# Linear attention on TensorE: from two streams to four, with head features, scores and state product in other pieces

## The chip, the cores and the metric

The kernel runs on one core of a Trainium2 chip. The metric is the time on the device in microseconds (us); lower is better. Everything is float32.

## What is computed

The program is a two-layer network over x of 8 batches, 1024 tokens and 128 features. The first layer (a recurrent mixer and a mixture of experts) and the gather of weight tiles that closes the second layer are the same before and after. The change is in the attention of the second layer, which runs three times over (L=3), causally over 1024 tokens, with 16 heads of 8 features, and then a feed-forward part of width 512:

```python
h = _layernorm(x, axis=-1) * (1 + ca) + sa
# favor(x, omega), 8 features out of 8 for each head
xs = x * dh ** (-0.25)
u = jnp.einsum('bshd,dm->bshm', xs, omega)
h = 0.5 * jnp.sum(xs * xs, axis=-1, keepdims=True)
return jnp.concatenate([jnp.exp(u - h), jnp.exp(-u - h)], axis=-1) * m ** (-0.5)
# one layer
q = (out @ Wq[l] + bq[l]).reshape(B, S, N_HEAD, dh)   # k, v likewise
Qf = favor(q, omega[l])
Kf = favor(k, omega[l])
a = causal_linear_attention(Qf, Kf, v).reshape(B, S, D)
a = a @ Wo[l] + bo[l]
h = layer_norm(out + a, ln1_g[l], ln1_b[l])
y = jax.nn.relu(h @ W1[l] + bf1[l]) @ W2[l] + bf2[l]
out = layer_norm(h + y, ln2_g[l], ln2_b[l])
```

## The kernel before

The attention works in 48 jobs. A job is one layer for 512 tokens (half a batch, four blocks of 128). Its running sum over tokens (`carry`) goes on to the other half of the batch, and its output to the next layer. Two streams s=0 and s=1 hold the buffers of two jobs (`at_xn0`, `at_xn1`, ...), and jobs of the two streams take turns. Every engine runs a hand-written sequence, `slot(a, f, then)`, once for each pair of jobs: job a does its first half (projections, features, sums, scores, weighting), the job before it, f, its second half (output projection, first layer norm, feed-forward, second layer norm), and `then` is the job that comes next. Engines meet by semaphores (`wait_ge`, `then_inc`); PSUM has eight banks of 128x512, four for each stream.

In one job, with the names of the buffers:

- TensorE turns the input (`transposed_input`, L1840, `at_xn`); ScalarE copies it out as `at_xT` (L1679). The first matmul of the slot, keys, is L1928; values L1929. Each is one matmul of 128x128 by 512 columns, which the profile shows as two records (x2).
- Head features: `omega` is folded into Wk and Wq once at the start (`feature_weights`, `at_wu`), so that u is one full matmul from `at_xT` (L1934, L1937 or L1938 for the queries' side) and minus the half square another with the constant `half` on `at_sqk` or `at_sqq`. With two matmuls for each of keys and queries these are four of 512 columns. ScalarE takes the exponential; queries come in four masked copies (L1669, `at_qa`), keys as `at_kb` by four products with masks on VectorE (L1543).
- `sums` (L1847): products of keys by token with values in tiles of 32x32. VectorE picks the blocks of a head out of them (L1553, state terms) and runs the prefix sum over the blocks (L1559).
- `scores` (L1859) come in two halves with half of `feed_forward_out` (L1890) after each; `causal` (L1565) masks each on VectorE. `carried` (L1868), the state product, is queries times state in two tiles of 64x64 on the diagonal, and `weighed` (L1875) scores times values, each half after its `causal`. VectorE divides (L1519) and turns the result.
- `output_weights` (L1882), sum and first layer norm (L346, L349, L368), feed-forward in four matmuls (L1965) and out in sixteen (L1890), second sum (L1576) and layer norm, whose output is the input of the job of the next layer, two slots later. Of layer 0 the input is the modulated layer norm of x instead; all of its steps were on VectorE.

After the last job, VectorE prepares the gather stage (`tiles_ahead`: L1460, L1442) in slot 48 and GpSimd writes the last rows (L1763 to L1769); tile rows are then loaded, normalised (L1637) and multiplied.

## Time and profile before

| | |
|---|---|
| median of 3 runs | 1801.85 us (1801.15 to 1805.26) |
| span of the profiled execution | 1828.0 us, granted TensorE clock 0.916 in the mean |
| TensorE matmul busy | 1571.7 us (86% of the span) |
| VectorE busy | 1443.5 us (79%) |
| ScalarE busy | 935.3 us (51%) |
| GpSimd busy | 698.6 us (38%) |

The runs are timed without the profiler; the profiled execution's own time is its span, 1828.0 us, 1.5% over the median. The attention's jobs lie from 520 us to about 1740 us of it. Busy is time in which at least one instruction runs; the rest is waiting or issue.

### The profile page before, as it was taken

How to read it: one execution, taken by the hardware profiler on the slowest of the kernel's cores; microseconds unless marked ns; L12 is line 12 of the kernel's file. 1: busy time of each engine (PE TensorE's matmuls, PEld its weight loads, DVE VectorE, ACT ScalarE, POOL GpSimd, SP SyncE). 2: the span in 40 equal slices, each digit the busy share in tenths (PEclk: the TensorE clock that was granted, in tenths of full speed). 3: DMA queues.
4: the chain of work that ended last, by engine and by line, in shares of the span. 5: the costliest groups of instructions: out<-in, count | busy, mean ns of one | idle time of the engine just before them, and what ended most of it. 6: DMA issues, size and time to landing. Idle time of an engine off the chain costs nothing.

```text
span 1828.0 us, 65037 instructions
## 1 busy us (share of the span) xinstructions
PE 1571.7 (86%) x27934; PEld 1150.5 (63%) x27934; DVE 1443.5 (79%) x3906; ACT 935.3 (51%) x1958; POOL 698.6 (38%) x620
## 2 busy tenths in 40 slices
PE   6777365399969999999999999999999999999853
PEld 4344254399946677776667777666677667777542
DVE  4998566766658888888888888888888988888864
ACT  4887476366524444445544444554444544444373
POOL 0777636345513234215224323423321522431354
PEclk9888655599969999999999999999999999999876
DMA  9730012333200000000000000100000000000437
GB/s 264 145 100 1 21 50 90 97 102 101 83 13 14 3 9 9 15 3 14 15 3 13 16 3 8 20 3 9 9 15 3 14 15 3 11 6 3 109 102 233
DMA packets 88606, 79.69 MB, mean 44 GB/s; under 512 B 22416, under 2 KB 77040, under 8 KB 88064
## 3 DMA queue, kind: packets, MB, share of 16 engines
q1 hardware_dynamic: 70736, 46.17, 9.6%
q0 software_dynamic: 10848, 25.70, 4.9%
q8 instruction: 221, 3.62, 0.9%
q10 hardware_dynamic: 6736, 3.66, 0.7%
q14 instruction: 65, 0.53, 0.1%
HBM read 46.74 MB, written 34.01 MB: 44 GB/s over the span
## 4 chain that ended last, share of the span: by engine, by line
PE 50%; DVE 13%; ACT 4%; issue 2%; DMA 1%; DVEq 1%; POOL 0%; another core or an unknown queue 0%; POOLq 0%; ACTq 0%
PE psum L1965 8%; PE psum L1890 8%; PE psum L1859 4%; PE psum L1868 4%; PE psum L1928 2%; PE psum L1934 2%; PE psum L1882 2%; PE psum L1936 2%; PE psum L1875 2%; PE psum L1937 2%; PE psum L1938 2%; PE psum L1948 2%; PE psum L1847 2%; DVE at_kb L1543 2%; PE psum L1929 2%
## 5 line engine op out<-in xcount | busy, mean ns | idle before, releaser
L1890 PE MATMUL psum<-attn_w,at_qa 128*128 128x128 f32 x1536 | 197.6, 282 | 0.0
L1752 POOL TENSOR_TENSOR at_xres<-at_xn,attn_rows 128x512 f32<-128x512 f32 x32 | 40.9, 1277 | 394.2 <-DVE at_xn L368 394.2
L1965 PE MATMUL psum<-at_vT,attn_w 128*128 128x512 f32 x384 | 180.6, 614 | 6.8 <-ACT at_vT L1697 5.8
L1890 PEld LDWEIGHTS psum<-attn_w,at_qa 128*128 128x128 f32 x1536 | 179.6, 192 | 6.1 <-issue 0.7
L1543 DVE TENSOR_SCALAR at_kb<-at_kf,const 128x512 f32<-128x512 f32 x192 | 178.4, 989 | 0.0
L1757 POOL TENSOR_TENSOR at_xn<-at_sqk,attn_rows 128x512 f32<-128x512 f32 x48 | 63.6, 1326 | 202.8 <-DVE at_sqk L368 202.8
L1549 DVE STREAM_TRANSPOSE at_vb<-at_vT 32x512 uint32<-32x512 uint32 x192 | 134.7, 701 | 1.9
L1669 ACT ACTIVATE at_qa<-at_qf,const 128x512 f32<-128x512 f32 x192 | 127.6, 714 | 1.6
L1713 ACT ACTIVATE at_qa<-psum,attn_bf 128x512 f32<-128x512 f32 x192 | 122.1, 678 | 10.6 <-PE psum L1965 5.4
L1565 DVE TENSOR_TENSOR at_weights<-psum,const 128x1024 f32<-128x1024 f32 x96 | 115.6, 1204 | 11.3 <-PE psum L1859 11.3
L361 ACT ACTIVATE at_rstd<-at_mv,const 128x4 f32<-128x4 f32 x96 | 28.1, 292 | 184.3 <-DVE at_mv L349 184.2
L1965 PEld LDWEIGHTS psum<-at_vT,attn_w 128*128 128x128 f32 x384 | 70.0, 192 | 82.2 <-issue 71.8
L1859 PE MATMUL psum<-at_qa,at_kb 64*64 64x64 f32 x6144 | 113.5, 224 | 9.5 <-issue 5.4
L1859 PEld LDWEIGHTS psum<-at_qa,at_kb 64*64 64x64 f32 x6144 | 100.5, 137 | 21.0 <-issue 9.9
L1868 PE MATMUL psum<-at_state,at_qa 64*64 64x36 f32 x3072 | 111.1, 242 | 0.0
L1868 PEld LDWEIGHTS psum<-at_state,at_qa 64*64 64x64 f32 x3072 | 106.3, 143 | 0.0
L1058 POOL DMA_INDIRECT token_y<-ex_y,ex_place x71 | 70.1, 988 | 85.3 <-DVE ex_y L1018 79.0
L1763 POOL TENSOR_TENSOR at_qf<-at_qf,ga_rows 128x512 f32<-128x512 f32 x16 | 20.3, 1271 | 207.8 <-DVE at_qf L368 207.8
L1847 PEld LDWEIGHTS psum<-at_v,at_kt 32*32 32x32 f32 x6144 | 62.1, 103 | 50.9 <-issue 49.4
L1049 POOL DMA_INDIRECT sorted_x<-ex_rows,ex_pos x64 | 63.2, 988 | 63.8 <-ACT ex_rows L1098 44.8
L346 DVE BATCH_NORM_STATS2 at_stats<-at_kt 128x6 f32<-128x128 f32 x384 | 83.8, 281 | 3.3
L1875 PE MATMUL psum<-at_vb,at_weights 128*32 128x36 f32 x6144 | 79.1, 201 | 8.1 <-issue 7.9
(308 smaller groups left out, 3884.2 us busy)
## 6 DMA issues: line engine op xcount, KB each, us to landing
ex_rows<-sorted_x SPq DMA_DIRECT2D x71, 129.0 KB
ti_rows<-tile_rows SPq DMA_DIRECT2D x8, 640.0 KB
x<-in_L_attn_x SPq DMA_DIRECT2D x8, 512.0 KB, 7.3
tile_rows<-in_L_attn_x SPq DMA_DIRECT2D x8, 512.0 KB
x<-token_y POOLq DMA_DIRECT2D x8, 512.0 KB
tile_y<-ti_rows SPq DMA_DIRECT2D x16, 192.0 KB
out<-x ACTq DMA_DIRECT2D x12, 256.0 KB
expert_w<-in_L_ffn_w SPq DMA_DIRECT2D x1, 2048.0 KB, 14.2
```

The lines of the kernel that those rows point to most:

```text
L346: nc.vector.bn_stats(stats[:, c, :], x_of(c))
L1543: last = nc.vector.tensor_scalar(kb[s][:, :, b, :], kf[s][:].rearrange("p (j i) -> p j i", i=SUB), cst(k, "mask_b")[:, b:b + 1], None, ALU ...
L1549: last = nc.vector.transpose(vb[s][q, :, :, b, 0:DH].bitcast(U32), vT[s][q, :].bitcast(U32).rearrange("p (j a d) -> p j a d", a=HQ, d=DH))
L1565: nc.vector.tensor_tensor(weights[a.s][:, i, :, :, :, :].rearrange("p h j a i -> p (h j a) i"), pair(a.s, 1 - i).rearrange("p (g i) -> p g ...
L1669: last = nc.scalar.activation(qa[s][:, :, i, :], qf[s][:].rearrange("p (j i) -> p j i", i=SUB), ACT.Copy, scale=cst(k, "mask_a")[:, i:i + 1])
L1713: nc.scalar.activation(hidden[f.s][:, t, :], bank(f.s, t), ACT.Relu, bias=k.bf1[:, f.l, t:t + 1]).then_inc(hid_taken, 1)
L1847: last = mm(bank(s, j)[quad(r), c * GW:(c + 1) * GW], kt[s][quad(j), c, quad(r)], v1[s][quad(j), c, :, r, :], start=True, stop=True)
L1859: last = mm(pair(s, 1 - i)[half_of(e), h * G + j * P // 2:h * G + (j + 1) * P // 2], kb[s][half_of(h), g, 2 * e:2 * e + 2, :].rearrange("p ...
L1868: mm(bank(1 - s, 2 + g // 8)[half_of(h), g % 8 * GW:(g % 8 + 1) * GW], qa[s][half_of(h), g, 2 * h:2 * h + 2, :].rearrange("p a i -> p (a i)"),
L1875: last = mm(bank(1 - s, 2 + i)[quad(a), g % 8 * GW:(g % 8 + 1) * GW], weights[s][:, i, a // 2, g % 8, a % 2, :], vb[s][:, g, a, :, :].rear ...
L1890: last = mm(bank(f.s, 1)[:, c * D:(c + 1) * D], hidden[f.s][:, t, c * P:(c + 1) * P], k.w2[:, f.l, t, :], start=(t == 0 and c == 0), stop= ...
L1965: mm(bank(f.s, c), k.w1[:, f.l, c * P:(c + 1) * P], hT[f.s][:], start=True, stop=True).then_inc(hid_ready, 1)
```

## The change

- **Four streams.** Job n belongs to stream n mod 4, so that the next layer of the same tokens comes four jobs later, not two. PSUM and most buffers are still by job parity; `at_xn` exists four times. Each slot holds three jobs on TensorE, `slot(a, p, f)`: a is job n with projections, features and sums; p is n-1 with scores, state product, weighting, output projection and first norm; f is n-2 with the feed-forward; and VectorE and ScalarE have a fourth, g = n-3, whose second norm is finished. There are 51 slots in the place of 49. Jobs take the batches in another order, and the gather stage (`order`) follows.
- **Scores in one piece**, all 64 before the state product. **The state product** (`carried`) in two parts: each now uses all four 64x64 tiles, since the halves of the output partitions are exchanged for every other group of columns. For that Wq's columns and bq are loaded turned by 32, Wo has a second copy with its halves exchanged (`wo_turned`), and the queries' features sit turned by one block.
- **Head features in 32x32 tiles**: omega is no longer folded. Keys and queries are projected, copied and squared on ScalarE (`ks`, `qs`, `sqk`, `sqq`), and sixteen tile matmuls of 32 rows by 512 columns make the features: eight with `omega`, eight with `half`. Tiles of keys write bank 2, tiles of queries bank 3.
- **ScalarE** takes on `ks` and `qs`, two of the four key masks and the normalising of the modulated input. The queries' exponentials are taken out of PSUM with a bias that is -1e30 for heads that a copy leaves out, so that the exponential and its four masked copies are four operations in the place of five.
- In the end, VectorE copies tile weights in slot 48 and takes the tile statistics in slot 49.

The diff, cut to its core, ScalarE's and then TensorE's helpers:

```diff
+                def mod_normalise(h):
+                    act.wait_ge(mod_stats, h.turn * 2 + MOD_SHIFTED)
+                    if h.group:
+                        act.wait_ge(outcome_free, h.turn - STREAMS + 1)
+                    for c in range(GC):
+                        nc.scalar.activation(xn[h.t][:, c, :], k.x[:, h.chunk + c, :], ACT.Identity,
+                                             bias=xshift[h.s][:, c:c + 1], scale=xrstd[h.s][:, c:c + 1]).then_inc(mod_ready, 1)
+
...
+                def queries_in(a):
+                    act.wait_ge(kqv_ready, a.n * 3 + QUERIES)
+                    nc.scalar.activation(qs[a.s], bank(1 - a.s, 0), ACT.Identity, bias=col(BQ, a.l), scale=SCALE).then_inc(kqv_taken, 1)
+                    nc.scalar.activation(sqq[a.s], bank(1 - a.s, 0), ACT.Square, bias=col(BQ, a.l), scale=SCALE).then_inc(kqv_taken, 1)
+
+                def carried_in(a):
+                    nc.scalar.activation(state[a.s][:, :, 0], carry[a.l][a.t][:], ACT.Copy, scale=keep[:, a.half:a.half + 1]).then_inc(xT_taken, 1)
+
+                def key_features(a):
+                    act.wait_ge(feat_ready, a.n + 1)
+                    nc.scalar.activation(kf[a.s][:], bank(a.s, 2), ACT.Exp, bias=cst(k, "feature")[:, HQ:HQ + 1]).then_inc(feat_taken, 1)
+
+                def query_features(a):
+                    for i in range(HQ):
+                        last = nc.scalar.activation(qa[a.s][:, :, i, :], bank(a.s, 3).rearrange("p (j i) -> p j i", i=SUB), ACT.Exp,
+                                                    bias=cst(k, "feature")[:, i:i + 1])
+                    last.then_inc(feat_taken, 1)
+
...
+                def values(a):
+                    pe.wait_ge(xT_taken, a.n * 2 + XT_PLACED)
+                    if a.n > 2:
+                        pe.wait_ge(second_added, a.n - 2)
+                    mm(bank(a.s, 1), k.wv[:, a.l, :], xT[:], start=True, stop=True).then_inc(kqv_ready, 1)
+
+                def keys(a):
+                    mm(bank(a.s, 0), k.w4[:, WK, a.l, :], xT[:], start=True, stop=True).then_inc(kqv_ready, 1)
+
+                def queries(a, p):
+                    if p:
+                        pe.wait_ge(weight_ready, p.n * 2 + 2)
+                    mm(bank(1 - a.s, 0), k.w4[:, WQ, a.l, :], xT[:], start=True, stop=True).then_inc(kqv_ready, 1)
+
+                def values_turned(a):
+                    pe.wait_ge(kqv_taken, a.n * 5 + VALUES_IN)
+                    for c in range(GC):
+                        last = nc.tensor.transpose(bank(a.s, 1)[:, c * P:(c + 1) * P], vT[:, c * P:(c + 1) * P], ident)
+                    last.then_inc(vtok_ready, 1)
+
+                def head_features(a, table, of_keys, of_queries, start):
+                    for r in quads:
+                        o = (r + 1) % 4
+                        mm(bank(a.s, 2)[quad(r), :], table[quad(r), quad(r)], of_keys[quad(r), :], start=start, stop=not start, skip_group_check=True)
+                        last = mm(bank(a.s, 3)[quad(r), :], table[quad(o), quad(o)], of_queries[quad(o), :], start=start, stop=not start, skip_group_check=True)
+                    return last
+
+                def features(a, p):
+                    if p:
+                        pe.wait_ge(att_ready, p.n * 2 + 1)
+                    pe.wait_ge(kqv_taken, a.n * 5 + QUERIES_IN)
+                    head_features(a, k.omega[:, a.l, :], ks[a.s], qs[a.s], True)
+                    pe.wait_ge(kqv_taken, a.n * 5 + QUERIES_SQUARED)
+                    head_features(a, cst(k, "half"), sqk[a.s], sqq[a.s], False).then_inc(feat_ready, 1)
+
...
-
-                def carried(s):
-
-                    for g in range(NSUB):
-                        for h in two:
-                            mm(bank(1 - s, 2 + g // 8)[half_of(h), g % 8 * GW:(g % 8 + 1) * GW], qa[s][half_of(h), g, 2 * h:2 * h + 2, :].rearrange("p a i -> p (a i)"),
-                               state[s][half_of(h), :, g], start=(g % 8 == 0), stop=False, skip_group_check=True)
-
...
+                        pe.wait_ge(state_ready, p.n + 1)
+                        if p.n > 1:
+                            pe.wait_ge(hid_taken, (p.n - 1) * FT)
+                    else:
+                        pe.wait_ge(carried_first, p.n + 1)
+                    for j in range(GC):
+                        for c in (i, 3 - i):
+                            g = 4 * c + j
+                            for h in two:
+                                last = mm(bank(1 - p.s, 2 + c // 2)[half_of((h + c) % 2), g % 8 * GW:(g % 8 + 1) * GW],
+                                          qa[p.s][half_of(h), g, 2 * h:2 * h + 2, :].rearrange("p a i -> p (a i)"),
+                                          state[p.s][half_of(h), :, g], start=(i == 0 and j == 0), stop=False, skip_group_check=True)
+                    if i == 0:
+                        last.then_inc(carried_first, 1)
+
+                def weighed(p, i, part):
...
```

VectorE's slot as it now stands:

```python
def slot(a, p, f, g, then):
    if a:
        values_by_block(a)
    if p:
        divided(p, 0)
        divided(p, 1)
        turned(p, 0)
    if g:
        second_normalised(g)
    if p:
        turned(p, 1)
    if a:
        values_by_token(a)
    if then and then.l == 0:
        mod_statistics(then)
    if p:
        first_sum(p)
    if a:
        masked_keys(a)
    elif p:
        weights_copied(0)
    elif f:
        tile_statistics(0, range(TROWS))
        tile_means(0)
        tile_shift(0)
    if p:
        first_normalised(p)
    if then and then.l == 0:
        mod_shifted(then)
    if a:
        states(a)
    elif p:
        weights_copied(1)
    elif f:
        tile_statistics(1, range(TROWS))
        tile_means(1)
    if f:
        second_sum(f)
    if a:
        causal(a, 0)
    if f:
        second_statistics(f)
    if a:
        causal(a, 1)
```

TensorE's:

```python
def slot(a, p, f):
    if a:
        transposed_input(a)
        values(a)
        keys(a)
        values_turned(a)
    if p:
        scores(p, 0, 0)
        scores(p, 0, 1)
        scores(p, 1, 0)
        scores(p, 1, 1)
        carried(p, 0)
        weighed(p, 0, 0)
        carried(p, 1)
        weighed(p, 0, 1)
        weighed(p, 1, 0)
        weighed(p, 1, 1)
    if f:
        feed_forward_in(f, 0)
    if a:
        queries(a, p)
    if f:
        feed_forward_in(f, 1)
        feed_forward_in(f, 2)
    if a:
        features(a, p)
    if p:
        output_weights(p, 0)
        output_weights(p, 1)
    if f:
        feed_forward_in(f, 3)
    if a:
        keys_turned(a)
    if f:
        feed_forward_out(f, 0)
        feed_forward_out(f, 1)
    if a:
        sums(a, 0)
        sums(a, 1)
        sums(a, 2)
    if f:
        feed_forward_out(f, 2)
    if a:
        sums(a, 3)
    if p:
        middle_turned(p)
    if f:
        feed_forward_out(f, 3)
    if f and not a and not p:
        tile_turned(0)
        tile_turned(1)
```

How the instructions stand on two engines, at the end of a slot (the name's number is the buffer's stream). TensorE before, from the second half of `feed_forward_out` (L1890) of one job through scores (L1859), state product (L1868) and weighting (L1875) of the other to the next job's keys and values (L1928, L1929):

```order
L1890 MATMUL psum<-attn_w2,at_qa1 128x128 x8
L1859 MATMUL psum<-at_qa0,at_kb0 64x64 x32
L1890 MATMUL psum<-attn_w2,at_qa1 128x128 x8
L1859 MATMUL psum<-at_qa0,at_kb0 64x64 x32
L1868 MATMUL psum<-at_state0,at_qa0 64x36 x32
L1875 MATMUL psum<-at_vb0,at_weights0 32x36 x32
L1840 MATMUL psum<-const,at_xn1 128x128 x4
L1875 MATMUL psum<-at_vb0,at_weights0 32x36 x32
L1928 MATMUL psum<-at_xT1,attn_w 128x512
L1929 MATMUL psum<-at_xT1,attn_wv 128x512
L1882 MATMUL psum<-attn_w,at_sqq0 128x128 x4
L1934 MATMUL psum<-at_xT1,omega 128x512
```

The same stretch on TensorE after; L1899 is `transposed_input`, L1906 values, L1909 keys, L1919 the values turned, L1963 scores, L1980 state product, L1993 weighting, L2018 feed-forward in, L1914 queries, L1925 a tile of features:

```order
L1899 MATMUL psum<-const,at_xn_of1 128x128 x4
L1906 MATMUL psum<-at_xT,attn_wv 128x512
L1909 MATMUL psum<-at_xT,attn_w 128x512
L1919 MATMUL psum<-const,at_vT 128x128 x4
L1963 MATMUL psum<-at_qa0,at_kb0 64x64 x64
L1980 MATMUL psum<-at_state0,at_qa0 64x36 x16
L1993 MATMUL psum<-at_vb0,at_weights0 32x36 x16
L1980 MATMUL psum<-at_state0,at_qa0 64x36 x16
L1993 MATMUL psum<-at_vb0,at_weights0 32x36 x48
L2018 MATMUL psum<-at_hT,attn_w1 128x512
L1914 MATMUL psum<-at_xT,attn_w 128x512
L2018 MATMUL psum<-at_hT,attn_w1 128x512 x2
```

Input, values and keys of the new job now come ahead of the scores of the one before it, no feed-forward stands between the scores, and the weighting no longer has the next input inside it.

VectorE before, from the values by block (L1549) of one job to the first norm of the other; L1553 and L1559 are the state terms and prefix sum, L1565 `causal`, L1576 the second sum:

```order
L1549 STREAM_TRANSPOSE at_vb0<-at_vT0 32x64x8 x4
L1553 TENSOR_TENSOR at_state0<-psum,const 128x4x4x36
L1559 SCALAR_TENSOR_TENSOR at_state0<-at_resets,at_state0 128x612
L1565 TENSOR_TENSOR at_weights0<-psum,const 128x1024
L1576 TENSOR_TENSOR at_kt1<-psum,at_xn1 128x512
L346 BN_STATS at_stats1<-at_kt1 128x6 x4
L349 BN_AGGR at_mv1<-at_stats1 128x2 x4
L1565 TENSOR_TENSOR at_weights0<-psum,const 128x1024
L368 TENSOR_SCALAR at_xn1<-at_kt1,at_mv1,at_rstd1 128x128 x4
```

VectorE after, from the state terms (L1548) on; L1559 is the second sum, L1567 `causal`, L1501 values by block, L1508 to L1510 `divided`:

```order
L1548 TENSOR_TENSOR at_state0<-psum,const 128x4x4x36
L1554 SCALAR_TENSOR_TENSOR at_state0<-at_resets,at_state0 128x612
L1559 TENSOR_TENSOR at_kt1<-psum,at_xn0 128x512
L1567 TENSOR_TENSOR at_weights0<-psum,const 128x1024
L351 BN_STATS at_stats1<-at_kt1 128x6 x4
L354 BN_AGGR at_mv1<-at_stats1 128x2 x4
L1567 TENSOR_TENSOR at_weights0<-psum,const 128x1024
L1501 STREAM_TRANSPOSE at_vb1<-at_vT 32x64x8 x4
L1508 TENSOR_SCALAR at_den0<-psum 128x32
L1509 RECIPROCAL at_den0<-at_den0 128x32
L1510 TENSOR_TENSOR at_kf0<-psum,at_den0 128x256
L1508 TENSOR_SCALAR at_den0<-psum 128x32
```

The second sum has moved ahead of the first `causal`, and values by block and the division now follow the second `causal`, where values by block had stood ahead of the state terms.

## Rows read from the trace of the kernel before

**Rows 1.** Windows: length; busy us (records) of PE, PEld, DVE, ACT, POOL; clock; DMA share; GB/s.

```profile
100.00:200.00 100.00, 70.55 (x219) 38.87 (x217) 87.04 (x153) 75.33 (x132) 74.71 (x66) 0.85 0.06 18
...
546.50:575.80 29.30, 25.72 (x541) 18.76 (x529) 24.27 (x47) 11.57 (x22) 8.64 (x5) 0.94 0.01 3
...
800.00:1000.00 200.00, 195.98 (x4220) 139.87 (x4219) 173.03 (x426) 96.70 (x186) 68.28 (x56) 1.00 0.04 9
```

**Rows 2.** Timeline of TensorE, one slot: start, duration, engine, line, records.

```profile
995.84 1.13 PE L1928 MATMUL psum<-at_xT,attn_w 128*128 128x512 f32 x2 [0.17 <-ACT at_xT L1679]
...
1000.69 1.02 PE L1937 MATMUL psum<-at_xT,attn_w 128*128 128x512 f32 x2
1001.55 1.02 PE L1938 MATMUL psum<-at_xT,at_wu 128*128 128x512 f32 x2
...
1009.49 0.76 PE L1847 MATMUL psum<-at_v,at_kt 32*32 32x36 f32 x64
1010.18 2.05 PE L1890 MATMUL psum<-attn_w,at_qa 128*128 128x128 f32 x16
1012.17 1.16 PE L1859 MATMUL psum<-at_qa,at_kb 64*64 64x64 f32 x64
...
1016.22 2.31 PE L1868 MATMUL psum<-at_state,at_qa 64*64 64x36 f32 x64
...
1019.34 0.66 PE L1840 MATMUL psum<-const,at_xn 128*128 128x128 f32 x4
...
1020.87 1.13 PE L1928 MATMUL psum<-at_xT,attn_w 128*128 128x512 f32 x2 [0.17 <-ACT at_xT L1679]
```

**Rows 3.** Timeline of VectorE in the same slot.

```profile
1007.90 2.85 DVE L1549 STREAM_TRANSPOSE at_vb<-at_vT 32x512 uint32<-32x512 uint32 x4
1010.78 1.17 DVE L1553 TENSOR_TENSOR at_state<-psum,const 128x576 f32<-128x576 f32 x1
1011.99 1.43 DVE L1559 TENSOR_TENSOR_SCAN at_state<-at_resets,at_state 128x612 f32<-128x612 f32 x1
1013.40 1.23 DVE L1565 TENSOR_TENSOR at_weights<-psum,const 128x1024 f32<-128x1024 f32 x1
1015.42 0.69 DVE L1576 TENSOR_TENSOR at_kt<-psum,at_xn 128x512 f32<-128x512 f32 x1 [0.80 <-PE psum L1890]
1016.14 0.87 DVE L346 BATCH_NORM_STATS2 at_stats<-at_kt 128x6 f32<-128x128 f32 x4
...
1017.38 1.19 DVE L1565 TENSOR_TENSOR at_weights<-psum,const 128x1024 f32<-128x1024 f32 x1
...
1019.51 0.19 DVE L1519 TENSOR_SCALAR at_den<-psum 128x32 f32<-128x32 f32 x1
...
1020.95 0.15 DVE L1519 TENSOR_SCALAR at_den<-psum 128x32 f32<-128x32 f32 x1
```

**Rows 4.** Timeline of ScalarE in the same slot.

```profile
1020.04 0.78 ACT L1679 ACTIVATE at_xT<-psum,attn_cols 128x512 f32<-128x512 f32 x1 [2.00 <-PE psum L1840]
```

**Rows 5.** Timeline, start and end of the attention's jobs.

```profile
520.48 1.12 PE L1840 MATMUL psum<-const,at_xn 128*128 128x128 f32 x4 [3.06 <-DVE at_feature_bias L1607]
...
575.78 1.12 PE L1928 MATMUL psum<-at_xT,attn_w 128*128 128x512 f32 x2 [0.17 <-ACT at_xT L1679]
...
1689.35 0.82 PE L1840 MATMUL psum<-const,at_xn 128*128 128x128 f32 x4
...
1740.98 1.11 DVE L368 TENSOR_SCALAR at_qf<-at_kt,at_mv,at_rstd 128x128 f32<-128x128 f32 x4 [0.60 <-ACT at_rstd L362]
```

**Rows 6.** Timeline, around the last outcome and the gather stage.

```profile
1714.21 1.27 POOL L1763 TENSOR_TENSOR at_qf<-at_qf,ga_rows 128x512 f32<-128x512 f32 x1 [13.51 <-DVE at_qf L368]
...
1722.04 5.57 DVE L1460 COPY ti_weights<-tilesT 128x128 f32 x20 [0.44 <-issue]
...
1727.53 2.02 DVE L1442 BATCH_NORM_STATS2 ti_stats<-ti_rows 128x6 f32<-128x128 f32 x10
...
1743.53 1.65 ACT L1637 ACTIVATE ti_rows<-ti_rows,ti_shift,ti_rstd 128x128 f32<-128x128 f32 x4 [0.32 <-DVE ti_shift L1452]
```

689 lines of the change are left out of this document (336 added, 353 removed).

## The prediction

> **What bounds the kernel now.** I read the windows first. From 800 to 1000 us TensorE is busy 195.98 of 200 us at a granted clock of 1.00, VectorE 173.03, ScalarE 96.70 [rows 1]. The jobs from 520 us on are thus bound by TensorE, and VectorE has 27 us of slack in 200. Next the first and last jobs: the first input is turned at 520.48, the second keys' matmul after it comes at 575.78, the last input at 1689.35, and the last outcome is normalised at 1740.98 for 1.11 [rows 5]. The turning stands 1.53 before the keys' matmul (1019.34 to 1020.87) [rows 2]. So the first two slots take 575.78 - 1.53 - 520.48 = 53.8, the next 45 take 1689.35 - 574.25 = 1115.1, that is 24.78 each, and what follows the last turning takes 1742.09 - 1689.35 = 52.7. The slot in the timelines is a usual one: 1020.87 - 995.84 = 25.03.
>
> **Prices.** A matmul of 512 columns takes 0.86 (1000.69 to 1001.55), 1.02 with its end; 64 records of sums 0.69; half of feed-forward out, 16 records, 1.99 (1010.18 to 1012.17), of which I put 0.24 down to the switch of tile shape, since a record of 128 columns is a quarter of 0.43; 64 records of scores 1.09 of their 1.16; 64 of the state product about 2.24 of 2.31; four transposes 0.66, of which 0.44 is issue [rows 2]. On VectorE: values by block 2.88 (1007.90 to 1010.78), state terms 1.21, prefix sum 1.43, first causal 1.23 after the scores began, second sum 0.69, statistics 1.24, causal 1.19, one division with its end 1.06 of the 1.44 to the next (1019.51 to 1020.95) [rows 3]. ScalarE copies the input out in 0.78 [rows 4].
>
> **TensorE's own work.** The four full matmuls of the features, 3.44, go. Sixteen tile matmuls of 512 columns come. If all four row groups work side by side, eight of them (one table) take two full matmuls' time for four at a time, or one for eight at a time. The trace has no tile of 512 columns. From below: four tiles of 64x64 in scores share the array at 1.09/64 = 17 ns a record. From above: the state product, whose two row halves write one bank, takes 2.24/64 = 35 ns a record with only 36 columns against 64 [rows 2]. I take one 0.86 for each table, 1.72 in all, since scores' tiles are as many and come as mixed. The state product should fall from 2.24 to about 1.1 in four tiles. TensorE's work now is 24.78 x 195.98/200 = 24.3 a slot; 24.3 - 1.7 - 1.1 = 21.5 are left, so some 3 us a slot would be waits.
>
> **Who is waited for then.** I follow a slot by the new order. VectorE and TensorE hand over to each other four times:
>
> - VectorE: state terms 1.21, prefix sum 1.4, second sum 0.69: 3.3. Only then may TensorE start the values, since `values` waits for the second sum that empties its bank.
> - TensorE: values 0.86, keys 0.86, values turned 0.44 and a switch, scores to the start of the causal 1.23 and a switch: 3.7. VectorE stands in front of the causal.
> - VectorE: causal 1.19, statistics 1.24, causal 1.19, values by block 2.88, two divisions 2.1, turned 0.4: 9.1 with a release. State product and weighting lie under values by block, so what the exchanged halves save there (1.1) is worth nothing; it would cost from about 2 us more on.
> - TensorE: features 1.72 with a release 0.15 and a switch 0.2, output projection 0.87, feed-forward in 0.86, keys turned 0.44, half of feed-forward out 1.75, three sums 1.1 with switches, feed-forward out 0.87, last sum 0.6: 8.6. It starts with the turned result, for which `features` waits.
>
> The sum is 3.3 + 3.7 + 9.1 + 8.6 = 24.7. It counts the end of a matmul (1.02 - 0.86 = 0.16) at hand-overs where the price has it already, so I take 24.5 for a slot of layers 1 and 2. In the slots of layer 0, a third, ScalarE now normalises the modulated input: four such operations take 1.65 [rows 6], ahead of the copy that TensorE waits for, nearly all on the path: +1.4. The mean is 24.5 + 1.4/3 = 24.95, against 24.78 now: 45 x 0.17 = **+7.7**. TensorE's work falls by 3 us and the slot does not, because values by block and the divisions, which lay beside full matmuls, now lie between the scores and the features with too little beside them. The two key masks that leave VectorE and the queries' copies on ScalarE lie in waits; they weigh only if VectorE has none.
>
> **Start.** The first slot holds job 0 alone: turning 1.53, two matmuls 1.7, ScalarE's copies and squares beyond them 3, features 1.9, exponential and keys turned and copied 2, four sums 2.8, state terms and prefix sum 2.6: 15.5; I take 15.1. The second has no feed-forward but the same hand-overs: 23.9. Together 39.0 against 53.8: **-14.8**. The folding of omega ahead of it goes: **-0.5**.
>
> **End.** After the last turning come slot 47 whole (24.5), slot 48 with the last job's weighting and the tile weights' copies of 5.57 on VectorE in the gaps (24.6), and slot 49, with the sum of the last feed-forward behind the tile statistics, which wait for the rows of the job before: its norm, GpSimd's three products from 1714.21 on as now, the load, and 2.02 of statistics twice [rows 6]. I put that slot at 22.5. Together 71.6 against 52.7: **+18.9**.
>
> The sum is 7.7 - 14.8 - 0.5 + 18.9 = +11.3. The profiled execution becomes 1828.0 + 11 = 1839; it is 1.5% over the median, so I put the same +11 on 1801.85: **1812**. Slots are uncertain by 0.4 either way (19), the end by 8: the likeliest case's own range is 1785 to 1838.
>
> **The clock.** It is 0.85 where TensorE is busy 70.55 of 100, 0.94 at 25.72 of 29.30, and 1.00 at 195.98 of 200 [rows 1]; each is a mean over its two levels, 1.2 and 2.4 GHz. After the change TensorE is busy 21.5/24.95 = 86%.
>
> **Rivals.**
>
> - *TensorE stays the bound* (24%, the other side: faster). Should VectorE finish its 9.1 earlier, the slot falls towards TensorE's 21.5 and a wait of 1.0 for the turned input (1019.34 + 0.66 to 1020.87, less what overlaps), about 22.5: 48 x 2.45 = 118 under the first case, 1694. The place is the wait of `values` for the second sum, and of `features` for the turned result; it decides once the mean slot is under 24.7. Half-way, at 23.7, it is 1752. For it: VectorE has 13% of slack now. Against it: the chain above adds only prices that rows show.
> - *Tiles of features don't run together* (13%). The tiles of four row groups write the same two banks. In the trace the one matmul whose row tiles share a bank is the slow one, 35 ns a record. If half run together, features take 3.44 in place of 1.72, on the path: +1.72 x 48 = +83, 1895. If only one per bank does, 6.9: +248, 2060. Against it: the state product reads its operand with a stride, which would explain it as well.
> - *The clock falls* (12%). Between the two lower points above, 86% gives 0.93. TensorE's parts of the chain are 3.7 + 8.6 = 12.3: +0.9 a slot, 48 x 0.9 = +44, 1856; at the 0.85 of the first row +2.2 a slot, 1916. Against it: each wait of the chain above is short, and the 0.94 follows a start from rest.
> - Others 5%; the hand-over chain 46%.
>
> The Trainium skill, "TensorEngine Tiling (Array Packing)", section "Gotcha 1: PSUM Pressure", says that different row tiles cannot access the same PSUM bank simultaneously. By it the second rival is true and the time 1895 or more; the 35 ns above agrees, but no run here separates the bank from the stride.
>
> **How the numbers follow.** No change means within 0.2%, 1798 to 1805.5. Of the first case a quarter lies under it (0.12), 0.07 in it, the rest over it. Faster: 0.24 + 0.12 = 0.36. Same: 0.09 with some of the others. Slower: 0.27 + 0.13 + 0.12 and the rest: 0.55. For 8 in 10 the range takes the upper half of the first rival, the clock and the milder form of the tiles: 1750 to 1896.
>
> **What would show it.** The distance from one `values` to the next is near 24.5 in layers 1 and 2, 26 in layer 0. TensorE is busy about 86% of the middle; its waits end by VectorE's second sum and turned result, and VectorE's longest wait by the scores. The sixteen tile matmuls take about 1.9. The state product takes about 1.1, unfelt. From the last turning to the last outcome are about 72 us. The clock stays over 0.98. I am wrong if TensorE stays busy over 95% (then the slot is its work), if features take 3 us or more, or if the clock in the middle is under 0.95.

## Result and profile after

The changed kernel takes **1982.6 us** (1976.1 to 1985.9, 4 runs) against 1801.5 of the kernel before beside it: 1.101 times as long, interval 1.098 to 1.104, 181 us more. The forecast was 1812, range 1750 to 1896. The direction was right, the size was not.

The page of the changed kernel (span and instructions; busy time by engine):

```profile
span 1974.3 us, 67718 instructions
...
PE 1533.6 (78%) x29056; PEld 1075.8 (54%) x29056; DVE 1340.0 (68%) x3767; ACT 1018.7 (52%) x2163; POOL 733.8 (37%) x620
```

The forecast's sign against itself came up: it said that it is wrong if the clock in the middle is under 0.95. Windows of the changed kernel, with the columns of [rows 1]:

```profile
800.00:1000.00 200.00, 166.68 (x3850) 111.90 (x3848) 135.32 (x351) 98.94 (x199) 74.86 (x58) 0.91 0.06 13
1200.00:1400.00 200.00, 167.59 (x3853) 112.24 (x3851) 133.85 (x333) 95.64 (x188) 59.69 (x44) 0.91 0.05 11
```

Where TensorE was busy 195.98 of 200 us at a clock of 1.00 it is now busy 167, at 0.91. VectorE is busy 135 of 200, less than before: no engine sets the time by its own work, they wait for each other. The first turning is at 498.8, which is 21.7 earlier than in [rows 5], of which 20 lie in the experts, whose last scatter starts at 480.29 and not 500.34: the profiled execution of before was that much slower there. From the first turning to the end it is 1974.3 - 498.8 = 1475.5 against 1307.5, 168 more.

TensorE's timeline, slot of job 18 (to compare with [rows 2]):

```profile
1000.16 2.04 PE L1906 MATMUL psum<-at_xT,attn_wv 128*128 128x512 f32 x2 [3.74 <-DVE at_kt L1559]
1001.99 1.92 PE L1909 MATMUL psum<-at_xT,attn_w 128*128 128x512 f32 x2
1003.70 1.06 PE L1919 MATMUL psum<-const,at_vT 128*128 128x128 f32 x4
1004.69 2.27 PE L1963 MATMUL psum<-at_qa,at_kb 64*64 64x64 f32 x128
1006.79 0.70 PE L1980 MATMUL psum<-at_state,at_qa 64*64 64x36 f32 x32
1007.42 0.47 PE L1993 MATMUL psum<-at_vb,at_weights 128*32 128x36 f32 x32
1007.82 0.74 PE L1980 MATMUL psum<-at_state,at_qa 64*64 64x36 f32 x32
1008.49 0.38 PE L1993 MATMUL psum<-at_vb,at_weights 128*32 128x36 f32 x18
1010.46 0.93 PE L1993 MATMUL psum<-at_vb,at_weights 128*32 128x36 f32 x78 [1.59 <-issue]
1011.32 1.13 PE L2018 MATMUL psum<-at_hT,attn_w 128*128 128x512 f32 x2
...
1015.11 0.61 PE L1925 MATMUL psum<-at_weights,omega 32*32 32x512 f32 x1
...
1016.47 0.59 PE L1926 MATMUL psum<-at_weights,const 32*32 32x512 f32 x1
1016.99 0.49 PE L2003 MATMUL psum<-attn_w,at_attT 128*128 128x128 f32 x2
...
1025.19 0.66 PE L1899 MATMUL psum<-const,at_xn 128*128 128x128 f32 x4
1028.40 1.44 PE L1906 MATMUL psum<-at_xT,attn_wv 128*128 128x512 f32 x2 [2.55 <-DVE at_kt L1559]
```

Four things stand here. Values waits 3.74 for the second sum (L1559). Behind the wait two matmuls start 1.83 apart (1000.16, 1001.99) where 0.86 is the price: the granted clock is at its lower level, 1.2 in place of 2.4 GHz, until the values are turned (1003.70 to 1004.69 for 0.6). Among the small matmuls of the weighting there is a gap of 1.59 that ends by "issue" (TensorE waited for nothing that the views show), between matmuls of the same form. What it waited for is shown below. And the sixteen tile matmuls of the features take 1015.11 to 1016.99, 1.88: they run eight records at a time, four tiles of each of the two banks, and the forecast 1.72 with its switch was right. The state product takes 0.63 + 0.67 in place of 2.24.

VectorE in the same slot, first causal (L1567), result turned (L1514), state terms (L1548), prefix sum (L1554) and second sum (L1559):

```profile
1006.11 1.23 DVE L1567 TENSOR_TENSOR at_weights<-psum,const 128x1024 f32<-128x1024 f32 x1 [6.10 <-PE psum L1963]
...
1014.61 0.45 DVE L1514 STREAM_TRANSPOSE at_attT<-at_kf 128x256 uint32<-128x256 uint32 x1
...
1023.99 1.17 DVE L1548 TENSOR_TENSOR at_state<-psum,const 128x576 f32<-128x576 f32 x1 [1.53 <-PE psum L1949]
1025.19 2.48 DVE L1554 TENSOR_TENSOR_SCAN at_state<-at_resets,at_state 128x612 f32<-128x612 f32 x1
1027.59 0.66 DVE L1559 TENSOR_TENSOR at_kt<-psum,at_xn 128x512 f32<-128x512 f32 x1
```

GpSimd at the end of the slot, the two products of the residual:

```profile
1025.12 1.26 POOL L1817 TENSOR_TENSOR at_xres<-at_xn,attn_rows 128x512 f32<-128x512 f32 x1
1026.46 2.27 POOL L1818 TENSOR_TENSOR at_xres<-at_xres,attn_rows 128x512 f32<-128x512 f32 x1
```

The prefix sum takes 2.48 for its 1.43 of [rows 3], and the second product 2.27 for 1.26, where they overlap. The first product started 0.07 ahead of the prefix sum and kept its 1.26. The second sum (L1559) reads one operand from PSUM and kept its 0.66 beside the second product. Over all 48 jobs the prefix sum's mean is 2.32.

Cutting each slot of the trace at the forecast's four hand-overs gives this table. The means are over the 44 slots from job 3 on, from the starts and ends of those same rows; the forecast's row is for layers 1 and 2. "Late" is from VectorE's turned result to the first matmul of features, which the forecast put at nothing. The lower rows are the experiments of the next section.

| us | values to causal | causal to turned | late | features to state terms | state terms to next values | slot |
|---|---|---|---|---|---|---|
| forecast | 3.7 | 9.1 | 0 | 8.6 | 3.3 | 24.7 |
| changed kernel | 4.64 | 8.98 | 1.38 | 8.82 | 4.35 | 28.16 |
| its five shortest slots | 3.69 | 8.94 | 0.05 | 8.70 | 4.35 | 25.75 |
| second sum first | 3.79 | 8.99 | 1.64 | 8.85 | 2.82 | 26.08 |
| GpSimd later | 3.89 | 9.00 | 1.75 | 8.84 | 3.52 | 27.00 |
| scores split | 2.89 | 9.55 | 0.69 | 8.80 | 4.36 | 26.29 |
| two unused matmuls | 3.68 | 9.03 | 1.99 | 9.00 | 4.31 | 28.02 |
| scores row broken | 4.19 | 9.09 | 1.32 | 8.98 | 4.26 | 27.85 |
| all three edits | 2.29 | 9.29 | 0.81 | 8.80 | 2.82 | 24.01 |
| its five shortest | 2.29 | 9.19 | 0.05 | 8.70 | 2.72 | 22.95 |

One of the short slots begins with these rows (TensorE, 1112.72 to 1138.47 = 25.75), at the full clock:

```profile
1112.72 1.10 PE L1906 MATMUL psum<-at_xT,attn_wv 128*128 128x512 f32 x2 [2.50 <-DVE at_kt L1559]
1113.65 1.02 PE L1909 MATMUL psum<-at_xT,attn_w 128*128 128x512 f32 x2
...
1138.47 2.05 PE L1906 MATMUL psum<-at_xT,attn_wv 128*128 128x512 f32 x2 [2.50 <-DVE at_kt L1559]
```

So the chain was the right one, to 0.2 us in three of its parts. Three terms came on top: the hindered prefix sum (1.0), the lower clock from values to scores (0.9), and TensorE late for the features (1.4).

Waits of TensorE from 700 to 1650 us (us in all, times, longest), the changed kernel:

```profile
PE psum L1906 <- DVE at_kt L1559: 74.8, 31, 3.8
PE psum L1993 <- issue: 36.0, 24, 1.9
PE psum L1980 <- issue: 20.4, 20, 1.6
PE psum L1963 <- issue: 9.8, 9, 1.5
PE psum L1925 <- DVE at_attT L1514: 7.4, 11, 1.0
```

"Issue" comes to 66 us in 950, about 2 a slot; the profiled execution of before has 11 in the same window.

**What ends the gaps marked issue.** The page has two DMA queues of the kind "instruction". Of this one every packet has 16 KB:

```profile
q8 instruction: 230, 3.77, 0.8%
```

From 700 to 1650 us 145 of these packets start, one for every 253 records of TensorE's matmuls and weight loads, so I take them for TensorE's own instructions, as they are loaded. One of them runs from 1007.75 to 1009.05, and the gap above ends at 1010.46, 1.41 us later. All 53 gaps marked issue from 700 to 1650 us end between 1.20 and 1.60 us after the end of such a packet, though these stretches are only 6% of the time. In the 15 profiles of the changed kernel and its variants taken where the kernel before runs in 1800 to 1802 there are 720 such gaps in that window, and all end between 1.18 and 1.61 after one (in the profiled execution of before 14 of 27 do, and the rest, at its sums and scores, stay unexplained). TensorE waits for its instructions to be loaded. The row of small matmuls has 242 records and as many weight loads in 4.2 us, which is 256 in 2.2 us. A packet takes 0.88 to 1.49, and TensorE goes on 1.20 to 1.60 later, 2.1 to 3.1 in all: as long as the row's use of 256 records or longer.

**The lower clock stands in two places.** One is behind the wait of values, in 27 of the 44 slots. The other is behind the gaps marked issue, as here in the slot of job 29:

```profile
1320.10 0.81 PE L1993 MATMUL psum<-at_vb,at_weights 128*32 128x36 f32 x34 [1.93 <-issue]
1320.84 2.08 PE L2018 MATMUL psum<-at_hT,attn_w 128*128 128x512 f32 x2
1322.70 1.92 PE L1914 MATMUL psum<-at_xT,attn_w 128*128 128x512 f32 x2
1324.41 2.67 PE L2018 MATMUL psum<-at_hT,attn_w 128*128 128x512 f32 x4
```

The clock's record has the lower level from 1319.16 to 1325.98, and the four matmuls ahead of the features take 6.2 us (1320.84 to 1327.01) where those of job 18 take 3.8 (1011.32 to 1015.11). This second place comes in 16 of the 44 slots. In them "late" is 3.14 in the mean and the gaps come to 2.58; in the other 28 it is 0.36 with gaps of 1.57. So most of "late" lies in slots in which a gap is followed by the lower clock. An estimate from these means: of the 2.78 between the two groups 1.0 are the longer gaps and 1.8 the clock, which is 0.6 a slot over all 44.

### The profile page after: what moved, and what is told of

It is laid out like the page before. It is cut to its first block, busy times and chain, and to the rows that moved or that the text cites. A ratio compares the mean times of both kernels' runs of the same rounds, so it can differ in the third digit from the quotient of the medians.

```text
span 1974.3 us, 67718 instructions
## 1 busy us (share of the span) xinstructions
PE 1533.6 (78%) x29056; PEld 1075.8 (54%) x29056; DVE 1340.0 (68%) x3767; ACT 1018.7 (52%) x2163; POOL 733.8 (37%) x620
## 4 chain that ended last, share of the span: by engine, by line
PE 45%; DVE 13%; issue 10%; ACT 4%; DMA 1%; POOL 0%; DVEq 0%; POOLq 0%; ACTq 0%; SPq 0%
PE psum L2018 7%; PE psum L2025 6%; PE psum L1963 4%; PE psum L1925 4%; PE psum L1906 4%; PE psum L1909 3%; PE psum L1949 3%; PE psum L1993 3%; DVE at_state L1548 2%; PE psum L2003 2%; DVE at_vb L1501 2%; DVE at_weights L1567 2%; PE psum L1980 2%; PE psum L1914 2%; PE psum L1919 2%
## 5 line engine op out<-in xcount | busy, mean ns | idle before, releaser
L1567 DVE TENSOR_TENSOR at_weights<-psum,const 128x1024 f32<-128x1024 f32 x96 | 116.1, 1211 | 232.3 <-PE psum L1963 232.2
L2018 PE MATMUL psum<-at_hT,attn_w 128*128 128x512 f32 x384 | 216.6, 670 | 3.2 <-ACT at_qa L1758 3.2
L1906 PE MATMUL psum<-at_xT,attn_wv 128*128 128x512 f32 x96 | 70.3, 822 | 107.4 <-DVE at_kt L1559 101.2
L1501 DVE STREAM_TRANSPOSE at_vb<-at_vT 32x512 uint32<-32x512 uint32 x192 | 134.6, 701 | 2.0
L1993 PE MATMUL psum<-at_vb,at_weights 128*32 128x36 f32 x6144 | 86.3, 206 | 55.3 <-issue 55.2
L1963 PE MATMUL psum<-at_qa,at_kb 64*64 64x64 f32 x6144 | 108.3, 225 | 11.9 <-issue 11.9
L1731 ACT ACTIVATE at_qa<-psum,const 128x512 f32<-128x512 f32 x192 | 115.8, 691 | 0.0
L1963 PEld LDWEIGHTS psum<-at_qa,at_kb 64*64 64x64 f32 x6144 | 100.2, 140 | 24.5 <-issue 24.3
L1554 DVE TENSOR_TENSOR_SCAN at_state<-at_resets,at_state 128x612 f32<-128x612 f32 x48 | 111.3, 2318 | 1.6
L2018 PEld LDWEIGHTS psum<-at_hT,attn_w 128*128 128x128 f32 x384 | 73.2, 213 | 63.6 <-issue 55.6
L1993 PEld LDWEIGHTS psum<-at_vb,at_weights 128*32 128x32 f32 x6144 | 70.5, 115 | 68.3 <-issue 58.4
L1710 ACT ACTIVATE at_vT<-psum,attn_bias_v 128x512 f32<-128x512 f32 x48 | 33.0, 687 | 140.3 <-PE psum L1906 140.3
L1548 DVE TENSOR_TENSOR at_state<-psum,const 128x576 f32<-128x576 f32 x48 | 56.2, 1170 | 64.9 <-PE psum L1949 64.9
L1980 PE MATMUL psum<-at_state,at_qa 64*64 64x36 f32 x3072 | 78.5, 242 | 27.0 <-issue 27.0
L1529 DVE TENSOR_TENSOR at_kt<-psum,at_xres 128x512 f32<-128x512 f32 x48 | 33.2, 692 | 90.2 <-PE psum L2003 90.1
```

What stands on the lines that cost most here:

```text
L1501: last = nc.vector.transpose(vb[a.s][q, :, :, b, 0:DH].bitcast(U32), vT[q, :].bitcast(U32).rearrange("p (j a d) -> p j a d", a=HQ, d=DH))
L1548: nc.vector.tensor_tensor(state[s][:, :, 1:SLOT].rearrange("p w (c j) -> p j c w", j=4), banks(s, 0, 4)[:, :, 0:GC * GW].rearrange("p j (c ...
L1554: nc.vector.tensor_tensor_scan(whole, resets[:].rearrange("p w j -> p (w j)"), whole, 0.0, ALU.mult, ALU.add).then_inc(state_ready, 1)
L1567: nc.vector.tensor_tensor(weights[a.s][:, i, :, :, :, :].rearrange("p h j a i -> p (h j a) i"), pair(a.s, 1 - i).rearrange("p (g i) -> p g ...
L1731: last = nc.scalar.activation(qa[a.s][:, :, i, :], bank(a.s, 3).rearrange("p (j i) -> p j i", i=SUB), ACT.Exp, bias=cst(k, "feature")[:, i ...
L1906: mm(bank(a.s, 1), k.wv[:, a.l, :], xT[:], start=True, stop=True).then_inc(kqv_ready, 1)
```

## Experiments

Each was run beside the kernel before, which took 1800 to 1802, but 1830 beside four of them, named below. Medians are of 4 to 10 runs, ratios are to the kernel before beside them. In the cut code, conditions (`if a.n > 2:` and the like) are left out.

### Undoing or moving one thing

**Second sum first** (`e1`). VectorE:

```diff
 if a:
     states(a)
 if f:
     second_sum(f)
 if a:
+    prefix(a)
     causal(a, 0)
```

`prefix` is the prefix sum, until here the second half of `states`.

> The second sum is placed between the state terms and the prefix sum on VectorE; nothing else of the changed kernel is altered. In the changed kernel the slot from one values matmul to the next is 28.2 us in the mean, TensorE waits 2.5 to 3.7 us for the second sum, and in most slots the clock is at its lower level for some 2 to 5 us after it. Theory A (this wait, and the lower clock behind it, are the loss): the sum is ready 2.4 us earlier and the input's copy is then what TensorE waits for, 1.2 us; 1.3 to 1.5 us a slot from the wait and up to 2.4 more from the clock, 1800 to 1915 in place of 1982. Rival B (the wait only moves: the prefix sum now delays causal and everything behind it): 1965 to 1990.

**1887.5** (ratio 1.046, 1.044 to 1.049): theory A. The last part of the slot falls from 4.35 to 2.82, and values no longer stands behind a wait that lowers the clock (4.64 to 3.79).

**GpSimd later** (`e2`).

```diff
     pool.wait_ge(*a.input[-1])
+    if a.n:
+        pool.wait_ge(state_ready, a.n)
```

> GpSimd's two products for the residual of a job wait for the prefix sum of the job before. In the changed kernel they run beside the prefix sum, which takes 2.32 us in the mean against 1.43 in the kernel before, while the product itself takes 2.27 in place of 1.27. Theory A (the two engines hinder each other): the prefix sum falls to 1.45, the slot by 0.9, 48 x 0.9 = 43 us less, 1940, or more where the shorter wait keeps the clock up. Rival B (the prefix sum is longer for its place or operands): it stays at 2.3 and the time within 5 us of 1982.

**1927.0** (1.067, 1.063 to 1.072): theory A. The second product, a mean of 2.27 in 32 of the changed kernel's jobs, is back at 1.26. The group of the prefix sum, its mean from 2318 down to 1560 ns:

```profile
L1554 DVE TENSOR_TENSOR_SCAN at_state<-at_resets,at_state 128x612 f32<-128x612 f32 x48 | 74.9, 1560 | 1.6
```

**Full features** (`e4`):

```diff
-    for r in quads:
...
+    mm(bank(a.s, 2), table, of_keys, start=start, stop=not start)
+    return mm(bank(a.s, 3), table, of_queries, start=start, stop=not start)
```

> The sixteen 32x32 tile matmuls of the head features are replaced by four full matmuls of 512 columns on the same operands (the queries' features are then not turned by a block, so that part of the result is another; the work of all engines is the same but for this). Theory A (the tiles save 3.44 - 1.72 = 1.72 on the path): +1.72 x 48 = +83, 2065. Rival B (they are not on the path, or the busier TensorE keeps its clock): within 10 us of 1982 or below.

**2030.1** (1.130, 1.124 to 1.135), +47: between A and B. The tiles save, but little over half of 83. The wait of values for the second sum falls from 74.8 to 43.6 us in 950, so part of the longer work may lie in it; that this is the reason isn't shown.

**Scores split** (`e6`). TensorE:

```diff
     values(a)
+    scores(p, 0, 0)
+    scores(p, 0, 1)
     keys(a)
     values_turned(a)
-    scores(p, 0, 0)
-    scores(p, 0, 1)
     scores(p, 1, 0)
```

> On TensorE the first half of the scores comes ahead of keys and the values turned, the second half after them; the changed kernel otherwise. VectorE's first causal waits for the first half alone. Theory A (VectorE's chain from causal on sets the slot): causal starts 1.4 us earlier (keys 0.86, turning 0.5), more at the lower clock: 48 x 1.4 to 2 = 67 to 96 less, 1885 to 1915. Theory B (TensorE's instructions are not delivered fast enough in the unbroken row of small matmuls, gaps marked issue of up to 2 us, 71 us of 1000): the row is broken in two, gaps fall below half. Rival C (TensorE's end of the slot sets it, whatever causal does): within 10 us of 1982.

**1888.4** (1.050, 1.047 to 1.052): theory A, and B with it. Causal starts 1.75 earlier in the mean (4.64 to 2.89); of the gaps marked issue, 28 of 66 us in 950 are left, and "late" halves. One edit moves both, so it doesn't share the gain out between them.

### The clock and the gaps apart

**Filler** (`e3`, three unused 512-column matmuls behind the wait for the input's copy) and **filler before the copy** (`e5`, two, ahead of it):

```diff
+    pe.wait_ge(sum_taken, a.n)
+    for _ in range(2):
+        mm(bank(1 - a.s, 2), k.wv[:, a.l, :], k.w1[:, a.l, :], start=True, stop=True)
     pe.wait_ge(xT_taken, a.n * 2 + XT_PLACED)
```

> Three matmuls of 512 columns, whose result is not used, are put on TensorE in the wait ahead of values, after the state terms; all waits of the useful work stay. Theory A (the lower clock after the wait is a loss of its own): the clock stays at its upper level at values, keys and scores, the mean slot falls from 28.2 by 1.5 to 2.4, 1865 to 1910. Rival B (the clock follows something else than this wait): nothing gained, and the three matmuls cost 0 to 0.5 a slot, 1982 to 2005.

> Two unused matmuls of 512 columns on TensorE as in the filler run before, but placed ahead of the wait for the input's copy, on constant operands, so that they end 0.8 us before values may start and delay nothing; the changed kernel otherwise. In the run with three of them behind that wait the clock in the middle was 0.98 against 0.91, yet values started later and the mean slot was 28.5. Theory A (the lower clock costs about 2 us a slot by itself): the clock is 0.96 or more and the mean slot 26.3 to 27.2, 1895 to 1940. Rival B (the lower level only fills time that TensorE would wait anyway): the clock rises but the time stays, 1970 to 1990.

The code is that of `e5`. `e3` gave **1989.3** (1.105, 1.103 to 1.106) at a clock of 0.98: values started later, as the expectation of `e5` tells. `e5` gave **1968.5** (1.090, 1.084 to 1.096): 14 us less, just below rival B's range and far from A's. Its window and waits:

```profile
800.00:1000.00 200.00, 173.63 (x3898) 115.10 (x3896) 138.45 (x354) 99.90 (x201) 79.38 (x61) 0.97 0.06 12
```

```profile
PE psum L1997 <- issue: 55.4, 37, 2.1
PE psum L1910 <- DVE at_kt L1559: 20.8, 25, 2.0
PE psum L1984 <- issue: 17.5, 15, 1.7
PE psum L1967 <- issue: 15.7, 12, 1.8
```

The clock is 0.97 for 0.91, and values to causal falls to 3.68, by the full 0.96. But "late" grows from 1.38 to 1.99, and issue gaps from 66 to 89 us in these rows, each still behind a packet of instructions. That the row meets its gap sooner because it starts sooner and at the full clock is argued, not shown. So the lower clock behind values costs 0.9 a slot, and taking it away gives back 0.3 (14 us in 48 slots). The second place of the lower clock isn't touched by this edit: it comes in 21 of the 44 slots now, and "late" is 3.14 in these and 0.94 in the others. `e5` therefore doesn't say what the clock costs in all.

**Row broken** (`e8`, then `g2`):

```diff
     scores(p, 0, 1)
+    unused(p)
     scores(p, 1, 0)
     scores(p, 1, 1)
+    unused(p)
```

`unused` is one matmul of 512 columns into a bank that the state product overwrites.

> The changed kernel with one unused matmul of 512 columns after each half of the scores, 1.7 us of TensorE more in each slot, so that the row of small matmuls (scores, state product, weighting) is broken twice. Theory A (instructions aren't delivered fast enough in a long row of small matmuls): gaps marked issue fall from some 71 us in 1000 to under 35, and the time stays or falls: 1940 to 1990. Rival B (the gaps have another cause): they stay, and the 1.7 comes on top where TensorE is late: 2000 to 2060.

> The changed kernel with an unused matmul after each half of the scores, where the kernel before takes 1800. In layers 1 and 2 its slots were 27.8 and 27.7 against 28.4 and 27.5 of the changed kernel. If late instructions cost about what the 1.7 us of unused work do, the time is 1975 to 1990 with half of the gaps. If they cost nothing, it is 1982 + 48 x 1 to 1.7 = 2030 to 2064.

`e8` ran where the kernel before took **1830**, and gave 2035.7 (1.113). `g2`, the same kernel beside a kernel before of 1802, gave **1968.1** (1.094, 1.091 to 1.096): 1.7 us more work in each slot, and 14 us less time. Its waits:

```profile
PE psum L1906 <- DVE at_kt L1559: 74.8, 34, 3.8
PE psum L1998 <- issue: 23.9, 26, 1.8
PE psum L1954 <- issue: 4.5, 5, 1.1
```

Issue falls to 28 us in these rows, 32 with the smallest. The gaps come from the length of the row of small matmuls. The 14 us of time are another matter, since the unused matmuls raise the clock too: 0.98 from 800 to 1000 us for 0.91. The lower level is gone behind the gaps in all 44 slots and stands at values in 14 in place of 27. By the table values to causal gains 0.45 and "late" only 0.06, though 1.7 us of work are put in ahead of it. `e5` at nearly the same clock (0.97) takes the same time without that work, and has 1.99 late for 1.32. So the shorter gaps and the clock behind them together pay for about the 1.7; this run doesn't part the two.

**Split and filler** (`e7`, then `g1`):

> The split scores (1888, clock 0.95 in the middle, few gaps marked issue) with the two unused matmuls ahead of values. In the changed kernel itself they raised the clock from 0.91 to 0.97 and gave only 14 us, but more gaps marked issue stood there. Theory A (the lower level behind the wait is a cost of its own where no gaps hide it; the split kernel has it in a fifth of its slots): clock 0.98 or more and 20 to 50 us less, 1840 to 1868. Rival B (it costs nothing even here): within 5 us of 1888.

> Split scores and two unused matmuls ahead of values, where the kernel before takes 1800. In layers 1 and 2 its slots were 26.3 and 26.0 in the disturbed run, against 26.5 and 26.2 of the split kernel. Theory A (the lower clock costs by itself): 1840 to 1868, slots of 25.3 to 25.8. Theory B (it fills time that is waited anyway): 1875 to 1892, slots within 0.3 of the split kernel's.

`e7`, beside the 1830, took 1954.9 (1.068). `g1` took **1874.6** (1.040, 1.037 to 1.043), 14 less than the split alone: values to causal 2.89 to 2.26, "late" 0.69 to 1.46, issue gaps 28 to 54 us in 950. The lower clock stands at values in 1 slot in place of 28. Theory B again, by the same exchange.

### Putting them together

> Both edits that gained: the second sum ahead of the prefix sum, and GpSimd's residual products behind the prefix sum. The second sum alone gave 1887.5 (mean slot 26.2, prefix sum still 1.84), the products alone 1927. If the two are one gain (both shorten the wait of values, which is now for the input's copy): 1880 to 1890. If the hindered prefix sum still counts, since it stands ahead of causal: 1887.5 - 48 x 0.4 = 1868. If they add: 1832.

**1878.2** (1.043, 1.037 to 1.048): 2 below the range of "one gain". The prefix sum falls from 1.84 to 1.45, which is 19 us in 48 jobs, and 9 of them reach the time.

> The two edits together with the split scores. If causal is what VectorE then waits for, its start 1.4 us earlier is worth another 48 x 1.4 = 67: 1800 to 1820, the time of the kernel before. If TensorE's own work and the input's copy now set the slot: 1855 to 1885.

**1788.4** (0.994, 0.992 to 0.996), and once more 1791.4 (0.995, 0.991 to 0.998): **0.5 to 0.6% under the kernel before**, a small gain, but both intervals lie under 1, and 194 us less than the changed one. Its window and waits:

```profile
800.00:1000.00 200.00, 182.10 (x4520) 125.08 (x4519) 148.53 (x394) 113.51 (x227) 65.82 (x54) 0.98 0.06 12
```

```profile
PE psum L1912 <- ACT at_xT L1708: 33.9, 39, 0.9
PE psum L1999 <- issue: 33.4, 26, 1.9
PE psum L1931 <- DVE at_attT L1514: 6.6, 13, 0.5
```

Values waits only for the input's copy, at most 0.9, and the clock is 0.98. The lower clock stands behind values in none of the 44 slots and behind a gap in 4.

**Full features and diagonal state product on top of it** (`d1`, `d2`), beside the 1830. `d1` has the edit of `e4`; that of `d2`:

```diff
-    last = mm(bank(1 - p.s, 2 + c // 2)[half_of((h + c) % 2), g % 8 * GW:(g % 8 + 1) * GW],
+    last = mm(bank(1 - p.s, 2 + c // 2)[half_of(h), g % 8 * GW:(g % 8 + 1) * GW],
```

> The kernel with all three edits (1788.4), but with the head features as four full matmuls of 512 columns in place of sixteen tile matmuls (the queries' features are then not turned by a block). On the changed kernel this cost 47 us, where 83 were worked out for a step wholly on the path. Theory A (features stand between VectorE's turned result and the sums): +1.72 x 48 = +83, 1871. Rival B (part of it is hidden as before): +45, 1833.

> The kernel with all three edits, but with the state product's halves not exchanged, so that it uses only the two tiles on the diagonal as in the kernel before (the second pair's result lands in the other half, so the output is another). It takes about 1.4 for 64 records now and should take 2.24. Theory A (it lies under values by block on VectorE): within 5 us of 1788. Rival B (feed-forward stands behind it and ahead of the features, and TensorE comes late there): +0.8 x 48 = +38, 1826.

1930.8 (1.055) and 1873.4 (1.025). These ratios can't be set beside 0.994: in all four kernels that ran beside the 1830, four slots of each twelve (job n with n mod 12 = 11, 0, 1 or 2, in which GpSimd scatters finished rows, mostly of layer 0) took 28 to 33, where they take 24.7 in the all-three kernel. In the other eight, which took 23.76 in the all-three kernel, `d1` takes 25.82, features to state terms 10.29 against 8.71: the tiles are worth 1.6 a slot, on the path, as the forecast had it. `d2` takes 23.92: the exchanged halves are worth 0.2 or less there, as it had it too. In `d2` the state product is back at 1.24 and 1.26 for 32 records each (from 1126.55), with the new order of the banks: the two tiles are what costs.

### What was different beside the 1830

TensorE's timeline in `d2`, the start of the sums in one of those slots:

```profile
860.16 0.53 PE L1955 MATMUL psum<-at_v,at_kt 32*32 32x36 f32 x37
860.93 0.28 PE L1955 MATMUL psum<-at_v,at_kt 32*32 32x36 f32 x5 [0.24 <-issue]
861.67 0.25 PE L1955 MATMUL psum<-at_v,at_kt 32*32 32x36 f32 x3 [0.47 <-issue]
862.42 0.25 PE L1955 MATMUL psum<-at_v,at_kt 32*32 32x36 f32 x4 [0.50 <-issue]
```

Four records come every 0.74 us, with a gap marked issue each time, from 860.9 to 864.6; GpSimd issues its four scatters from 858.9 to 863.9. These gaps aren't those of the changed kernel: of the 58 at the sums of `d2` from 700 to 1650 us only 5 end 1.0 to 1.75 after a packet of TensorE's instructions. The scatter was moved one slot later, ahead of the next slot's other work:

```diff
+    pool.wait_ge(out_ready, (g.n + 4) * 2)
     pool.wait_ge(outcome_free, g.turn + 1)
     for c in range(GC):
```

> The kernel with all three edits once more, as the reference of this call. Where the kernel before takes 1800: 1788 as before. Where it takes 1830 as in the last call and late instructions are the cause: layer-0 slots 29 to 29.5, 1788 + 20 + 14 x 4.5 = 1870, ratio 1.02.

> All three edits, and GpSimd scatters the finished rows one slot later, behind the weighting, where TensorE runs large matmuls and needs few instructions. Theory A (the scatter's transfers hold up TensorE's instructions in the sums): layer-0 slots fall to 24 to 25 wherever it runs; against the reference of this call 45 to 65 us less if that has the 29.5, and 0 to 10 less if not. Rival B (the layer-0 slots are long for the extra statistics and the normalising on ScalarE): within 5 us of the reference.

> The changed kernel with the scatter moved alone. Theory A: where the layer-0 slots are disturbed, 45 to 65 us less than the changed kernel; where not (28.8 in layer 0 against 28.4 and 27.5 in its profile), up to 10 less. Rival B: within 5 us.

> The changed kernel itself, so that the one above has its own reference on this chip. Where the kernel before takes 1800: 1982. Where it takes 1830: 2000 by the slower experts alone, 2045 with late instructions in the slots of layer 0.

The kernel before took 1800 beside these four, so the disturbed case didn't come up: 1791.4, **1801.5** (1.001, 0.999 to 1.003), **1977.1** (1.100, 1.097 to 1.102) and **1982.6** (1.102, 1.100 to 1.105). Where nothing is disturbed, moving the scatter gives nothing to the changed kernel and costs the other 10. What holds the instructions up in the other case isn't shown.

## Why the prediction failed

- **The chain of hand-overs** (values, causal, turned result, state terms) was right: 3.69, 8.94, 8.70 in the shortest slots against 3.7, 9.1, 8.6. The slot doesn't follow TensorE's own work, 21.5.
- **The prefix sum's price** failed: 1.43 was taken from [rows 3], where it ran alone. GpSimd's residual products now run beside it. The step priced VectorE and TensorE in their new places and left GpSimd out. It costs 1.0 a slot (4.35 for 3.3 in the last part); undone, -55 us. The Trainium skill, "SBUF — State Buffer", section "Terms", calls the port pair of the two engines exclusive and held for the full instruction; the rows agree: the first product, which started first, kept its 1.26, the prefix sum beside it took 1.05 longer, and the second product beside the prefix sum 1.01 longer.
- **"It starts with the turned result"** failed: that TensorE isn't late for the features was taken for granted and never priced, and it costs 1.38 a slot. Weighting and state product were put under values by block by their work, but their instructions are loaded too slowly, 2 us a slot, and four full matmuls (3.4) stand between them and the features, at the lower clock in 16 of 44 slots.
- **The clock** was a rival at 12% and +0.9 a slot, spread over all of TensorE's parts. It fell to 0.91 and costs 0.9 from values to causal alone, and by the estimate above some 0.6 more within "late". As a cause of the whole it would have been too small, and it isn't apart from the other two: the waits of values that it follows were 2.5 to 3.8, not short, and the hindered prefix sum's 1.0 is in them; the other low stretches follow the gaps. That the size named in the forecast met the first part was luck, since it was read off the busy share.
- **Layer 0** was put at +1.4 for the normalising on ScalarE, 0.45 in the mean slot. It isn't there: 28.04 against 28.21 in the other layers. The likely reason is that values waits for the second sum there, which ends later; where that wait is gone, with all three edits, it is 24.29 against 23.89, 0.4. So the slot is 3.5 over the 24.7 of the table but only 3.25 over the forecast's mean of 24.95.
- **Tiles of different rows in one bank** don't wait for each other: 1.88 for sixteen. That rival falls, and with it, for this kernel's time, the rule of the Trainium skill, "TensorEngine Tiling (Array Packing)", section "Gotcha 1: PSUM Pressure": no row of tiles waits for another, each writes other partitions of the bank. The old state product's 35 ns a record was due neither to the bank nor to the stride, since the new one has both and takes (0.63 + 0.67)/64 = 20 ns; with two tiles in place of four (`d2`) it is back at 35 to 39.
- **Start and end**: first values to third 44.2 in place of 39.0; from the last values to the end 159.9, against 137.1 before, +22.8 for +18.9. Nine of the 170. By the forecast's own marks the end missed by more: from the last turning (1811.29) to the last outcome (1892.60) are 81.3 for 71.6; the gather stage behind it is then 4 shorter than before (81.7 for 85.9).
- The sum: (28.20 - 24.95) x 45 = 146, start 5, end 4: 155 of the profile's 1974.3 over 1828.0 - 20 + 11 = 1819. The profiled execution is accounted for to 1 us; the median of the runs, 1982.6, is 8 higher than its span.
- **The rival "TensorE stays the bound"** needed a slot under 24.7. With three small moves the slot gets there, though TensorE at 182 of 200 us busy isn't the bound even then: 24.1 in the mean from the third slot on: 45 x 0.7 = 31 us less than [rows 5] give, 11 less at the start (first values to third 42.8), and 19 more at the end (155.9 for 137.1). The new end takes back almost half of what the new slots bring.
